# Masked cross-attention: one exponential over a head's 2048 keys instead of two over 1024

## What is computed

```python
scores = jnp.einsum('bhqd,bhkd->bhqk', qh, kh)
scores = jnp.where(mask[:, None, :, :], jnp.float32(-1000000000.0), scores) * scale
attn = jax.nn.softmax(scores, axis=-1)
out = jnp.einsum('bhqk,bhkd->bhqd', attn, vh)
out = out.transpose(0, 2, 1, 3).reshape(B, Sq, Hd)
return out @ Wo.T
```

## Time and profile before

| what | value |
|---|---|
| median of 3 runs | 1642.56 us (1642.55 to 1643.27) |
| the profiled execution, own time | 1643.34 us |
| its span (first to last instruction) | 1642.0 us |
| PE, ACT, DVE, POOL busy | 97%, 56%, 63%, 8% |
| granted TensorE clock, mean | 0.994 |
| exponentials (L1379) | 128 operations of 1157 ns, 148.1 us |
| the copies of turned blocks on ACT (L1387) | 192 of 586 ns, 111.1 us |
| mask and maximum on DVE (L1433) | 256 of 685 ns, 172.7 us |

### The profile page before, as it was taken

How to read it: one execution, slowest core, us unless ns; L and a number is a source line. 1 busy time by engine, 2 the same in 40 slices (tenths; PEclk the granted TensorE clock), 3 DMA queues, 4 the chain that set the end, 5 groups by cost and what they waited for, 6 DMA issues and landing times.

```text
span 1642.0 us, 29506 instructions
## 1 busy us (share of the span) xinstructions
PE 1593.5 (97%) x11286; PEld 1309.2 (80%) x11286; DVE 1033.3 (63%) x2257; ACT 922.2 (56%) x1730; POOL 132.3 (8%) x107
## 2 busy tenths in 40 slices
PE   7999999999999999999999999999999998999998
PEld 5778888887788878889988888887757877787776
DVE  5777777686564342555555565568665547797875
ACT  6666767664234422454555555578853346676764
POOL 0000000000000001100010001000064101010011
PEclk9999999999999999999999999999999998999999
DMA  6332323321760039988897887889950165798852
GB/s 242 121 103 90 94 87 94 99 69 60 280 210 4 11 111 309 339 250 258 249 269 228 261 260 236 251 229 241 312 194 7 43 266 174 261 328 302 304 175 67
DMA packets 147258, 307.48 MB, mean 187 GB/s; under 512 B 11452, under 2 KB 101564, under 8 KB 135548
## 3 DMA queue, kind: packets, MB, share of 16 engines
q1 hardware_dynamic: 145564, 300.60, 56.7%
q0 software_dynamic: 1536, 4.76, 1.0%
HBM read 224.11 MB, written 81.22 MB: 186 GB/s over the span
## 4 chain that ended last, share of the span: by engine, by line
PE 84%; DVE 6%; ACT 4%; issue 2%; DMA 2%; SPq 1%; DVEq 0%; POOL 0%; ACTq 0%; POOLq 0%
PE bank L128 16%; PE bank L130 16%; PE bank L129 16%; PE bank L1310 6%; PE bank L1332 3%; PE bank L2370 3%; PE bank L1300 3%; PE bank L2374 3%; PE bank L2371 3%; PE bank L2405 2%; DVE WS L2688 2%; PE bank L1836 2%; PE bank L1754 1%; PE bank L1821 1%; PE bank L487 1%
## 5 line engine op out<-in xcount | busy, mean ns | idle before, releaser
L1433 DVE CUSTOM_DVE_ANT_0 TT<-bank,MASK 128x512 f32<-128x512 f32 x256 | 172.7, 685 | 60.4 <-PE bank L1300 59.9
L2688 DVE TENSOR_TENSOR WS<-EW,WS 128x1024 fp32r<-128x1024 f32 (+1 forms) x144 | 161.6, 1132 | 45.5 <-ACT WS L2518 44.4
L2518 ACT CAST WS<-EW 128x1024 fp32r<-128x1024 f32 (+1 forms) x144 | 139.1, 977 | 50.4 <-PE bank L2374 48.9
L1387 ACT COPY PT<-bank 128x512 f32<-128x512 f32 x192 | 111.1, 586 | 96.5 <-PE bank L1310 96.2
L1310 PE MATMUL bank<-IDN,TT 128*128 128x128 f32 x1024 | 153.9, 274 | 1.7 <-ACT PT L1387 1.7
L128 PE MATMUL bank<-BCH,WKT 128*128 128x256 f32 x512 | 149.4, 292 | 4.2 <-DVE BCL L360 4.2
L1379 ACT ACTIVATE TT<-TT,MX 128x1024 f32<-128x1024 f32 x128 | 148.1, 1157 | 1.8 <-DVE MX L1439 1.2
L129 PE MATMUL bank<-BCL,WKT 128*128 128x256 f32 x512 | 145.1, 283 | 0.0
L130 PE MATMUL bank<-BCH,WKT 128*128 128x256 f32 x512 | 145.1, 283 | 0.0
L1310 PEld LDWEIGHTS bank<-IDN,TT 128*128 128x128 f32 x1024 | 121.7, 140 | 26.1 <-issue 7.5
L335 ACT CAST EKH<-bank 128x512 fp32r<-128x512 f32 x64 | 37.5, 586 | 160.6 <-PE bank L130 151.9
(11 more groups left out here) (345 smaller groups left out, 3784.3 us busy)
## 6 DMA issues: line engine op xcount, KB each, us to landing
EW<-in_ewg SPq DMA_DIRECT2D x48, 1024.0 KB, 6.4
KST<-tmp_k SPq DMA_DIRECT2D x43, 768.0 KB, 6.8
tmp_k<-EKH SPq DMA_DIRECT2D x128, 256.0 KB, 3.3
EW<-in_ewg SPq DMA_DIRECT2D x24, 768.0 KB, 5.2
CT<-in_ctxT SPq DMA_DIRECT2D x32, 512.0 KB, 3.4
CN<-in_ctxN SPq DMA_DIRECT2D x32, 512.0 KB, 3.5
BCT<-in_ctxT SPq DMA_DIRECT2D x32, 512.0 KB, 4.4
tmp_k<-EKL SPq DMA_DIRECT2D x64, 256.0 KB, 3.2
```

The costliest lines, as they stand in the source:

```text
L1387: act.copy(PT[:, g % NP], bank[turn_bank[g]][:]).then_inc(*p_act.up)
L1433: dve.tensor_tensor_reduce(TT[:, sl, 512 * kc:512 * kc + 512], bank[(0, 1, 4)[g % 3]][:], MASK[:, b % 2, 512 * kc:512 * kc + 512], 1.0, NE ...
L2518: act.copy(WS[:, i % NR, 0, 0:n * w], EW[q % NE][:, at:at + n * w]).then_inc(*w_high.up)
L2688: dve.tensor_tensor(WS[:, i % NR, 1, 0:n * w], EW[q % NE][:, at:at + n * w], f(WS[:, i % NR, 0, 0:n * w]), ALU.subtract).then_inc(*w_low.up)
```

## The change

All 2048 exponentials of a head are one operation, called where the first half was, in steps 0 and 4 of a pair, and it gives one sum. The tile `SUM` loses its last axis, the addition in `pair_sums` is gone, the semaphore `s_exp` counts 64 and not 128, and PE waits for a pair's exponentials once (step 0) and not twice (steps 0 and 4).

```diff
-        SUM = A("SUM", [128, 2, 16, 2])
+        SUM = A("SUM", [128, 2, 16])
...
-        s_exp, p_act, o_kept = S.new("act", 128), S.new("act", 192), S.new("act", 32)
+        s_exp, p_act, o_kept = S.new("act", 64), S.new("act", 192), S.new("act", 32)
...
-                if pc % 4 == 0:
-                    pe.wait_ge(*s_exp[2 * (2 * p + 1) + pc // 4])
+                if pc == 0:
+                    pe.wait_ge(*s_exp[2 * p + 1])
...
-                if kc % 2 == 0:
-                    b, h, cs = n // 16, n % 16, slice(512 * kc, 512 * kc + 1024)
-                    if kc == 0:
-                        act.wait_ge(*s_max[n])
-                    act.activation(TT[:, n % 4, cs], TT[:, n % 4, cs], ACT.Exp, bias=MX[:, n % 4, 5:6], scale=SC1,
-                                   accum_out=SUM[:, b % 2, h, kc // 2:kc // 2 + 1]).then_inc(*s_exp.up)
+                if kc == 0:
+                    b, h = n // 16, n % 16
+                    act.wait_ge(*s_max[n])
+                    act.activation(TT[:, n % 4, :], TT[:, n % 4, :], ACT.Exp, bias=MX[:, n % 4, 5:6], scale=SC1,
+                                   accum_out=SUM[:, b % 2, h:h + 1]).then_inc(*s_exp.up)
...
-                dve.wait_ge(*s_exp[2 * (2 * p + 1) + 1])
-                own(dve.tensor_reduce(RS[:, c:c + 2], SUM[:, b % 2, c:c + 2, :], AX.X, ALU.add))
-                dve.reciprocal(RS[:, c:c + 2], RS[:, c:c + 2]).then_inc(*sums_turned.up)
+                dve.wait_ge(*s_exp[2 * p + 1])
+                dve.reciprocal(RS[:, c:c + 2], SUM[:, b % 2, c:c + 2]).then_inc(*sums_turned.up)
```

## The result

The changed kernel takes 1659.3 us, median of 11 runs (1654.55 to 1662.8); the kernel before, in runs beside it, 1642.82 us (11 runs, 1641.53 to 1652.91). The ratio is 1.0079 with a 95% interval of 1.006 to 1.0097: 13.0 us longer, between 9.9 and 15.9. The forecast was 1648.9 us in a range of 1643.5 to 1653.5. The direction was right, the size was half of what came, and the range missed it.

The account below looks back on a forecast made before the run. TensorE bounds the whole (PE 97%); in masked cross-attention from 1083.5 us, 5 x 0.85 + 5 x 0.24 + 0.85 = +6.30 us on 1642.56 gives 1648.9 us, range 1643.5 to 1653.5.

Parts of the forecast that it names:

- The walk: Masked cross-attention from 1083.5 us: step-by-step delays of five short, five long and one last interval, +6.30 us in all.
- copy 5: ACT's copy of step 5, behind the odd head's exponential; claimed to start at 1118.40 instead of 1117.55 in the short interval.
- turn 0: PE's turn reusing the PSUM bank that copy 5 empties; claimed +0.85 us in short and last intervals, +0.24 in long.
- the first regime: Masked cross-attention, 680 to 1081 us, PE filled with background products; claimed change 0, bounds 0 and +20 us.
- DVE's saving: 32 reductions and the stops behind them go, about 0.18 us a pair; claimed worth nothing because DVE runs dry.
- ACT's 0.60 us a pair: Fall in ACT's own work over the eleven intervals from 1083.48 us; claimed no gain, as ACT only idles more.
- rival C: Larger loss: longer exponential, clock lost in PE's gap, or background work stalled; 1652.3 us, 1667 or up to +20; chance 0.10.
- PE's longer gap costs clock: Gap of about 1.1 us before turn 0 lowers PE's clock in each of 11 intervals: +18, 1667 us; within 0.10.
- A, ACT's load: Faster: ACT's load, not the maximum's moment, sets the stage from 1083.5 us; 6.6 us go, 1636.0 us; chance 0.08.
- B, an earlier maximum: No change: DVE's maximum early enough for the odd exponential to start right behind copy 4; +0.6, 1643.2 us; chance 0.10.
- C's first form: The merged exponential takes 2.31 us, nothing saved; +9.7 us, 1652.3 us; most of rival C's 0.10.
- C's third: The first regime stalls, background groups losing 0.85 us each; up to +20 us; within rival C's 0.10.

Follow-up runs that it names:

- a_fill4: The changed kernel plus four constant matmuls on TensorE in the gap of the five short intervals; 1648.79 us, 1.0046 against the kernel before.
- filled kernels: The changed kernel with eight, four or two constant matmuls in the gap of the five short intervals; 1654.32, 1648.79 and 1654.27 us.
- best2: Kernel before, even head's exponential merged, odd head's halves called in steps 5 and 6, except the very first odd head's first half, kept early; 1645.15 us, 1.0005.
- even_only: Kernel before with only the even head's exponentials merged (step 0), the odd head keeping two halves; 1647.44 us, 0.9999.
- halves_later: Kernel before, both halves kept, the first called one step later, in steps 1 and 5, behind their copy; 1648.12 us, 1.0025.
- best1: Kernel before with the even head's exponential merged at step 0 and the odd head's halves called in steps 5 and 6; 1645.01 us, 1.0011.
- after: The changed kernel itself, all 2048 exponentials of each head in one operation, first trace; 1659.3 us, 1.0079 against the kernel before.
- gap_only: Kernel before, nothing merged; in the later part ACT waits ahead of copy 5 for a later mask row; 1659.33 us, 1.0084.
- after2: The changed kernel run again word for word, second trace; 1661.1 us, 1.01 against the kernel before.

## Why the prediction was wrong

**The walk held.** Read at full clock, each of its steps came as written: the exponential at 2.00 us, its start 5.45 behind the batch, copy 5 two microseconds later, turn 0 0.70 behind it, 9.62 us per interval with no alternation, the first regime untouched, DVE's saving and ACT's 0.60 us a pair worth nothing. `a_fill4`, in which the clock holds, gives it in full: the intervals +6.5 us against +6.30, its time 7.6 us above the kernel before (5.3 to 9.9), where the forecast had 6.3.

**The step that failed** stands under rival C: "Or PE's longer gap costs clock". The gap had been foreseen (about 1.1 us; it is 1.07), and the price of a fall (1.7 us; 1.6 to 1.7). What was wrong was how the two were put together. I priced it as all or nothing, each of the 11 intervals or none, and gave the whole rival 0.10, "mostly its first form". In fact only six intervals have the long gap, and a part of those, three or four, bring a fall: some 5 to 7 us in the stage, not 18 and not 0. The forecast's own sum took the clock as 1.00 because the earlier trace rows shows 1.00 for the kernel before; but that row is of a stretch in which TensorE's idle times end at 0.22 us ahead of turn 0 and 0.49 us ahead of the score of step 7, and the change was about to make the first five times as long. The nearest evidence for the price of such a gap was the row for 665 to 670 us, and it was used for the price but not for a chance. With half of the six gaps taken as falls the forecast would have been 1642.56 + 6.3 + 3 x 1.6 = 1654, and with all six the range would have reached to 1659. That half is known only from the traces of the changed kernel.

**What is left.** That is still short of the 1659.3 measured. The profiled execution is at the low end of its runs (1655.95 of 1654.55 to 1662.8), and there +0.6 stood ahead of the first batch, which the walk did not have, and +0.7 behind the stage. For the rest there is the mean granted clock of the runs: 0.9948 with a mean time of 1645.8 us before, 0.9895 with 1659.0 us after. Time lost at the lower level is then 1645.8 x 0.0052 = 8.6 us against 1659.0 x 0.0105 = 17.4 us: 8.8 of the 13.2 us of difference are clock, 4.4 are the rest, which the walk puts at 6.3; the rows give the clock to a thousandth, 1.6 us, so this is rough. The table gives much the same: the three traces of the changed kernel lose 15.9 us on average over the whole execution, the two of before 6.9, which is 9.0 us apart: 5.7 in the stage, 0.5 ahead of it and 2.8 behind it, in self-attention and the experts (6.3 against 3.4). The mean clock of the filled kernels is back at 0.994 to 0.995, and they lose 1.7 to 1.8 us behind the stage, which suggests that the gaps have a part in that too; how they would reach a later stage whose code is the same is not shown, and `best2`, without such gaps, loses 6.9 there. So the 3 us behind the stage stay open.

**The rivals.** A, ACT's load: refuted by `even_only`; its rule was weighed in the prediction. The Trainium skill's Perfetto Trace Analysis, Optimizing Scalar/DVE Operations, ties the gain of larger operations to a saturated engine. By busy share ACT with 88% might pass for one; the trace shows it waiting 0.7 us for a maximum ahead of each odd exponential, and there the rule's second half, that smaller pieces may let work finish sooner, is what the runs show. Only where the order was changed so that ACT is late by itself, in `halves_later` against `best1`, may its load count, 0.3 us in a short interval. B, an earlier maximum: refuted, copy 5 slipped by the full 0.85. C's first form, 2.31 us: refuted by the row at 2010 ns. C's third, a stalled first regime: refuted by 400.94 of 401.00 us.

**Smaller misses.** The idle ahead of the score of step 7 grew a little as well (0.47 us in `after`). Of the experiments, `halves_later` came at 8.68 instead of 8.4 because copy 5, now ahead of the exponential, makes that start 0.43 us late, `gap_only` had one fall in each trace instead of two to five, and two of the falls of `after2` stood at their old places. The sign that was set for rival A, intervals below 9.06 us on average, was no sign: the average before is 8.99.

## What to carry over

Merging two operations on an engine that waits for its input makes the second one part of the path: ask what stands behind it in the queue and what that releases. A change that opens a gap on TensorE is priced twice, once as the gap and once as a chance of a stretch at the lower clock behind it, and that second term belongs into the sum and the range as soon as the new gap is longer than what stood at that place before. If such a gap can't be closed, a few matmuls of constants in it, shorter than the gap, may be cheaper than the falls; here four of them gave back 12 us by the medians of runs on one chip.

## What the runs showed of the hardware

The clock fell from 2.4 to 1.2 GHz and came back within about 3.4 us, in a stage in which PE is busy 97.50 of 110.00 us, behind idle of 0.47 and 1.07 us with one score between; each of the 15 falls lost 1.7 us. Longer idle of 1.48 us was followed by one in two cases of ten. What decides that is open.

In every kernel, the one before among them, falls come behind this stage, and in all but `best2` ahead of it too (in the kernel before at 410 and 665 us). An example behind it, in the kernel before:

```profile
1355.00:1360.00 5.00, 4.57 (x38) 4.23 (x37) 2.89 (x16) 2.09 (x3) 1.91 (x3) 0.96 0.00 0
1360.00:1365.00 5.00, 4.64 (x22) 4.65 (x22) 2.22 (x2) 0.72 (x1) 1.60 (x1) 0.50 0.23 67
```

The granted clock is 0.96 and then 0.50 with PE busy 4.6 of 5 us in both rows. Behind the stage the traces lose between 1.7 and 8.6 us to such stretches and ahead of it between 0 and 5.2, from one execution to the next, so a gain of 2 us in the stage, as in `best2`, drowns in them.
